# Block numbers of the expansion packed four to a word, one register load for 64 groups, column rows requested earlier

## The chip, the cores and the metric

The kernel runs on one core of one Trainium2 chip. The metric is the device time of one execution in microseconds (us); lower is better.

## What is computed

The reference is a three-layer graph network over N = 12,500 nodes with D = 128 features and E = 400,000 weighted edges.

```python
def _spmm(row, col, vals, x):
    msg = vals[:, None] * x[col]
    return jax.ops.segment_sum(msg, row, num_segments=N)

def _layer(x_prev, row, col, vals, W_a, b_a, W_b, b_b):
    h = _spmm(row, col, vals, x_prev)
    z = (h + x_prev) @ W_a.T + b_a + h * x_prev @ W_b.T + b_b
    return jnp.where(z >= 0, z, NEG_SLOPE * z)
x = emb[x_ids]
x1 = _layer(x, row, col, vals, W1_1, b1_1, W1_2, b1_2)
x2 = _layer(x1, row, col, vals, W2_1, b2_1, W2_2, b2_2)
x3 = _layer(x2, row, col, vals, W3_1, b3_1, W3_2, b3_2)
return jnp.concatenate((x, x1, x2, x3), axis=1)
```

## The kernel before

A preparation phase (the first third of the time) sorts the edges so that each layer can be computed with matmuls on blocks of 125 nodes, and writes small tables. Then a loop over the three layers (`with pe.Fori(0, LAYERS)`, line 956 on TensorE, and its like on the other engines) runs three stages after one another:

- **Expansion** (lines 960 to 973). The edges, ordered by the block of their source node, lie in 896 groups of 512 slots (GROUPS = 896, GE = 512). All edges of a group have their source in one block of 125 nodes. For a group TensorE makes the 512 messages as four tiles of 128 slots: each tile is a one-hot matrix of the column numbers (`col_hot`, the weights) times the block's features, which are split into three bf16 pieces (x_high, x_mid, x_low) summed in PSUM. So a group is 4 x 3 = 12 matmuls, each with its weight load. Which block a group uses is only known at run time. A loop body of AU = 16 groups (56 bodies a layer) begins with one instruction that loads 16 words from a table in SBUF (`group_at`, one word per group, already multiplied by D) into 16 registers of TensorE's sequencer (line 961), and each group's matmuls take their address from its register.
- Around it: SyncE loads the column numbers of 4 groups at a time (`load_cols`, line 636, one row of 4 KB, four rows in `col_src`), GpSimd spreads such a row to all partitions (line 556, into one of CR2 = 2 places in `col_row`), VectorE turns two groups at a time into one-hots (`make_hot`, line 1334, six groups ahead of use, a ring of OHR = 8 groups). PSUM has 8 banks, one group each. Of each pair of groups ScalarE multiplies the first by the edge values (line 745) and VectorE the second (line 1347) into a ring of MR = 8 message buffers, and SyncE stores each group, 128 x 512 fp32 = 256 KB, to memory (line 644).
- The order on SyncE's queue is written by hand in `store_messages`: before the stores of groups 0, 4, 8 and 12 of body i it waits for `col_spread[h]` (row h of body i has been spread, so its place in `col_src` is free) and loads row h of body i + 1.
- **Gather and sum** (lines 975 to 982): 592 tiles a layer; GpSimd gathers 128 rows of the stored messages by an indirect DMA (line 571), and TensorE sums them by rows with one-hot matmuls (line 980), a loop of 74 bodies of 8 tiles.
- **Dense** (lines 984 to 1018): the two weight matrices, the bias and the leaky step, written out for all 50 steps on TensorE without a loop, and the new features go to xb and to the output.

The tables are made once, in preparation: `start_groups` (line 1276) is written to memory as `group_offsets` by SyncE and read back as one row on partition 0 (lines 623 and 627).

Of the kernel before, what the change touches and what calls it, by code (L numbers as in the profile page):

```python
# [20 lines left out]
I32 = mybir.dt.int32  # L21
U8 = mybir.dt.uint8
ALU = mybir.AluOpType
# [3 lines left out]
P = 128  # L27
N = 12500
E = 400000
D = 128  # L30
LAYERS = 3
SLOPE = 0.2
DMA = 16
# [36 lines left out]
AU = 16  # L70
# [11 lines left out]
CR2 = 2  # L82
ABODIES = GROUPS // AU

CHB = 8
# [32 lines left out]
def graph_layers(nc, ids, row, col, vals, emb, weights, biases, out):  # L118
    ctx = ExitStack()
    with ctx:  # L120
# [6 lines left out]
        def dram(name, shape, dt=F32):  # L127
            return nc.dram_tensor(name, shape, dt, kind="Internal").ap()

        sorted_edges = [dram(f"sorted_edges{k}", [DUMPS[k] + SPARE, RUN * 2]) for k in range(2)]  # L130
        lane_places = dram("lane_places", [2, NBD, LT], BF16)
        group_offsets = dram("group_offsets", [P, GTW], I32)
        tile_rows = dram("tile_rows", [P, TBW], I32)
# [36 lines left out]
        iota_l = sb("iota_l", [P, TABW])  # L170
        start_groups = sb("start_groups", [P, GTW], I32)
        start_rows = sb("start_rows", [P, TBW], I32)
# [86 lines left out]
        base_of = work[:, TBL0 + TB:TBL0 + 2 * TB]  # L259
        group_at = wi[0:1, TBL0 + 2 * TB:TBL0 + 2 * TB + GROUPS]  # L260
        row_at = wi[0:1, TBL0 + 2 * TB + GROUPS:TBL0 + 3 * TB + GROUPS]
# [315 lines left out]
        def _(sp):  # L577
# [44 lines left out]
            sp.wait_ge(offsets_ready, 3)  # L622
            sp.dma_start(group_offsets, start_groups[:, :]).then_inc(offsets_stored, DMA)
            sp.dma_start(tile_rows, start_rows[:, :]).then_inc(offsets_stored, DMA)
            sp.dma_start(tile_base, start_base[:, :]).then_inc(offsets_stored, DMA)
            sp.wait_ge(offsets_stored, 3 * DMA)
            sp.dma_start(group_at, group_offsets.rearrange("p t -> (p t)")[0:GROUPS].rearrange("(a t) -> a t", a=1)).then_inc(offsets_in, DMA)
            sp.dma_start(row_at, tile_rows.rearrange("p t -> (p t)")[0:TB].rearrange("(a t) -> a t", a=1)).then_inc(offsets_in, DMA)
# [5 lines left out]
            with sp.Fori(0, LAYERS) as la:  # L634
                def load_cols(i, h):
                    sp.dma_start(col_src[h * 32:h * 32 + 1, :], cols_of[bass.ds(i * CB + h, 1), :]).then_inc(col_src_in[h], DMA)

                def store_messages(i, last):
                    for n in range(AU):
                        if n % BATCH == 0 and not last:  # L640
                            sp.wait_ge(col_spread[n // BATCH], la * ABODIES + i + 1)
                            load_cols(i + 1, n // BATCH)
                        sp.wait_ge(msg_ready[n % 2], la * (GROUPS // 2) + i * (AU // 2) + (ACREDIT + n // 2 + 1))
                        sp.dma_start(messages[bass.ds(i * (AU * P) + n * P, P), 0:CH * D], msg[:, n % MR, :]).then_inc(msg_stored[n % MR], DMA)  # L644

                for h in range(CB):
                    load_cols(0, h)
                with sp.Fori(0, ABODIES - 1) as i:
                    store_messages(i, False)
                store_messages(ABODIES - 1, True)  # L650
                with sp.Fori(0, DSTEPS // DU) as i:
                    for k in range(DU):
                        sp.wait_ge(xb_ready, la * DSTEPS + i * DU + (k + 2))
                        sp.dma_start(new_out[bass.ds(i * DU + k, 1), bass.ds(la + 1, 1), :, :, :].rearrange("a b r h d -> (a b r) h d"),
                                     xb[:, bass.ds(i * (2 * DU) + 2 * k, 2), :]).then_inc(x_stored, DMA)
# [138 lines left out]
        def _(pe):  # L794
# [161 lines left out]
            with pe.Fori(0, LAYERS) as la:  # L956
                pe.wait_ge(xb_ready, la * DSTEPS + 1)
                pe.wait_ge(pieces_ready, la * SPLITS + SPLITS)
                pe.sem_inc(pe_layers, 1)
                with pe.Fori(0, ABODIES) as i:  # L960
                    _, offs = nc.values_load_multi_w_load_instructions(
                        group_at[0:1, bass.ds(i * AU, AU)], engines=[mybir.EngineType.PE],
                        min_val=0, max_val=(NB - 1) * D, skip_runtime_bounds_check_because="the table holds offsets of blocks")
                    for n in range(AU):
                        if n % 2 == 0:
                            pe.wait_ge(col_hot_ready, la * (GROUPS // 2) + i * (AU // 2) + (n // 2 + 1))
                        pe.wait_ge(msg_ready[n % 2], la * (GROUPS // 2) + i * (AU // 2) + (n // 2 + 1))
                        for j in range(CH):
                            at = n % OHR * GE + j * P
                            for k, piece in enumerate((x_high, x_mid, x_low)):  # L970
                                last = t.matmul(ps[:, n % PR, j * D:(j + 1) * D], col_hot[:, at:at + P],  # L971
                                                piece[:, bass.ds(offs[n], D)], start=k == 0, stop=k == 2)
                        last.then_inc(expanded, 1)
# [47 lines left out]
        def _(dve):  # L1021
# [253 lines left out]
            blocks_of(iota_gt, GTW, ct[11][:, 0:NB], w[17][:, 0:GTW])  # L1275
            v.tensor_scalar(start_groups[:, :], w[17][:, 0:GTW], float(D), None, ALU.mult).then_inc(offsets_ready, 1)
            ask()
# [150 lines left out]
```

## Time and profile before

| | us |
|---|---|
| median of 3 runs | 8945.59 (8935.71 to 8948.48) |
| the profiled execution, its own time | 8948.78 |
| its span in the trace | 8947.1 |

```profile
PE 7924.2 (89%) x84296; PEld 7333.9 (82%) x84297; DVE 7107.3 (79%) x10046; ACT 4558.1 (51%) x14210; POOL 5595.2 (63%) x3638
PEclk8999995899996799999999999999999999999999
q8 instruction: 84, 1.38, 0.1%
PE 56%; DVE 5%; issue 3%; DMA 3%; ACT 1%; DVEq 1%; SPq 0%; POOL 0%; POOLq 0%; ACTq 0%
```

PE is TensorE's matmul side, PEld its weight loads, DVE VectorE, ACT ScalarE, POOL GpSimd. A q behind an engine's name is its sequencer or, for SP, its DMA queue. The first line gives busy time, share of the span and number of instructions; the second the granted clock of TensorE in 40 slices of the span, in tenths of full speed; the third the queue that carries instruction code (packets, MB, share of 16 engines); the last the shares of the chain that ended last. Register, branch and semaphore instructions are not counted as busy. A matmul's recorded end is modelled, so starts are the safer reading. In the rows of one line, a/b/c are the shortest, median and longest duration in ns, then the first and last start in us.

### The profile page before, as it was taken

The numbers are of one execution on the slowest core, as the hardware profiler recorded it, in microseconds if no ns is written. First come the engines' busy times: TensorE is split into PE (matmuls) and PEld (weight loads), VectorE is DVE, ScalarE is ACT, GpSimd is POOL, SyncE is SP. The second block draws the span as 40 slices with busy tenths as digits, with TensorE's granted clock in tenths as the row PEclk, the third lists the DMA queues.
The fourth block names the chain that finished last, engine by engine and source line by source line (L and its number), as shares of the span: only waits on it lengthen the run. The fifth ranks groups of instructions, "written<-read, shape, count | busy, mean of one in ns | idle before, by whom it ended". The sixth has DMA issues, their size and how long they took to land.

```text
span 8947.1 us, 257893 instructions
## 1 busy us (share of the span) xinstructions
PE 7924.2 (89%) x84296; PEld 7333.9 (82%) x84297; DVE 7107.3 (79%) x10046; ACT 4558.1 (51%) x14210; POOL 5595.2 (63%) x3638
## 2 busy tenths in 40 slices
PE   5999986799995688899999788899999788899999
PEld 4777775577773588799999788799999788899999
DVE  8999988799996877777777777777777777777777
ACT  0999990799993366611112566511112566511112
POOL 4788774588783233388886233488885333488884
PEclk8999995899996799999999999999999999999999
DMA  2111111211119988888886588888886688888885
GB/s 78 7 7 7 7 7 38 34 7 7 7 7 30 155 309 312 302 282 287 286 286 247 209 309 307 301 284 286 286 286 224 235 307 310 297 284 287 287 286 200
DMA packets 1005688, 1721.41 MB, mean 192 GB/s; under 512 B 378356, under 2 KB 429624, under 8 KB 1004920
## 3 DMA queue, kind: packets, MB, share of 16 engines
q0 software_dynamic: 378656, 958.17, 35.5%
q1 hardware_dynamic: 499680, 753.27, 23.7%
q10 hardware_dynamic: 127224, 8.24, 3.6%
q8 instruction: 84, 1.38, 0.1%
q14 instruction: 44, 0.36, 0.0%
HBM read 963.06 MB, written 756.12 MB: 192 GB/s over the span
## 4 chain that ended last, share of the span: by engine, by line
PE 56%; DVE 5%; issue 3%; DMA 3%; ACT 1%; DVEq 1%; SPq 0%; POOL 0%; POOLq 0%; ACTq 0%
PE ps L980 37%; PE ps L971 17%; DMA messages<-work 2%; DVE work L1334 2%; DVE hT L1297 1%; PE ps L1008 1%; PE ps L988 1%; PE ps L1009 1%; DVE work L1347 1%; ACT work L745 1%; SPq L644 0%; DVEq L1355 0%; PE ps L998 0%; DVE work L1321 0%; DVE hT L1359 0%
## 5 line engine op out<-in xcount | busy, mean ns | idle before, releaser
L980 PE MATMUL ps<-work 128*128 128x125 f32 x28416 | 3281.9, 278 | 45.8 <-DVE work L1363 45.5
L980 PEld LDWEIGHTS ps<-work 128*128 128x128 f32 x28416 | 3240.4, 192 | 87.2 <-DVE work L1363 46.9
L571 POOL DMA_INDIRECT work<-messages,work x1776 | 2708.8, 1525 | 615.9 <-issue 608.4
L971 PE MATMUL ps<-xb,work 125*128 x10752 | 1909.2, 222 | 450.8 <-DVE work L1334 426.3
L1363 DVE TENSOR_TENSOR work<-work,iota_p 128x1000 f32<-128x1000 f32 x1776 | 2120.0, 1194 | 0.4
L556 POOL PARTITION_BROADCAST work<-work x672 | 890.8, 1326 | 1854.9 <-DMA work<-slot_cols 903.6
L745 ACT ACTIVATE work<-ps,work 128x128 f32<-128x128 f32 x5376 | 1537.1, 369 | 960.4 <-PE ps L971 918.0
L971 PE MATMUL ps<-hT,work 125*128 x10752 | 1904.4, 221 | 0.0
L971 PE MATMUL ps<-work 125*128 x10752 | 1898.5, 220 | 0.0
L763 ACT ACTIVATE work<-work 128x8 f32<-128x8 f32 x1776 | 534.4, 301 | 2675.5 <-DMA work<-messages,work 2675.5
L870 PEld LDWEIGHTS ps<-hT 128*128 128x128 f32 x12768 | 1484.0, 196 | 297.1 <-ACT stage L668 227.3
L870 PE MATMUL ps<-hT 128*128 128x96 f32 x12768 | 1520.1, 280 | 186.6 <-ACT stage L668 186.3
L522 POOL DMA_INDIRECT sorted_edges<-stage,run_idx x798 | 1452.3, 1820 | 307.9 <-issue 237.5
L679 ACT ACTIVATE hT<-iota_p,place 128x128 f32<-128x128 f32 x5320 | 1580.2, 389 | 125.9 <-DVE place L1161 82.8
L971 PEld LDWEIGHTS ps<-xb,work 125*128 125x128 bf16 x10752 | 1047.0, 97 | 479.5 <-issue 479.5
L1347 DVE TENSOR_TENSOR work<-ps,work 128x512 f32<-128x512 f32 x1344 | 920.9, 685 | 636.0 <-PE ps L971 614.4
L1374 DVE TENSOR_TENSOR hT<-hT,ps 128x125 f32 x1776 | 505.8, 285 | 808.1 <-PE ps L980 808.1
L971 PEld LDWEIGHTS ps<-work 125*128 125x128 bf16 x10752 | 1046.6, 97 | 9.5
L971 PEld LDWEIGHTS ps<-hT,work 125*128 125x128 bf16 x10752 | 1052.4, 98 | 1.9
L1334 DVE TENSOR_SCALAR work<-work,iota_c 125x1024 bf16<-125x1024 bf16 x1344 | 885.8, 660 | 0.0
L1154 DVE TENSOR_REDUCE place<-ps 128x24 f32<-128x2400 f32 x266 | 706.5, 2656 | 110.1 <-ACT hT L682 96.6
L512 POOL TENSOR_TENSOR hT<-hT,work 128x672 f32<-128x672 f32 x266 | 363.2, 1366 | 428.6 <-DVE hT L1174 428.6
(212 smaller groups left out, 5680.8 us busy)
## 6 DMA issues: line engine op xcount, KB each, us to landing
messages<-work SPq DMA_DIRECT2D x2688, 256.0 KB, 3.2
work<-messages,work POOLq DMA_INDIRECT x1776, 5.9
out_x<-xb SPq DMA_DIRECT2D x150, 125.0 KB
sorted_edges<-stage,run_idx POOLq DMA_INDIRECT x798
work<-slot_cols SPq DMA_DIRECT2D x672, 4.0 KB
work<-lane_places SPq DMA_DIRECT2D x532, 5.2 KB, 2.1
out_x<-xb ACTq DMA_DIRECT2D x4, 1562.5 KB
sorted_edges<-hT SPq DMA_DIRECT2D x4, 908.0 KB
```

What stands on the lines that cost most here:

```text
L522: pool.indirect_dma_start(out=sorted_edges[p], out_offset=bass.IndirectOffsetOnAxis(ap=run_idx[:, q, k:k + 1], axis=0), in_=stage[:, q, k ...
L556: g.partition_broadcast(col_row[:, h % CR2, :], col_src[h * 32:h * 32 + 1, :], channels=P).then_inc(col_spread[h], 1)
L571: pool.indirect_dma_start(out=ck[:, n, :, :].rearrange("p h x -> p (h x)"), out_offset=None, in_=flat, in_offset=bass.IndirectOffsetOnAxis ...
L679: last = s.activation(to_part[q][:, k, :], iota_p[:, :], ACT.Abs, bias=place[:, q, 2, k:k + 1], scale=-1.0)
L745: last = s.activation(msg[:, n % MR, j * D:(j + 1) * D], ps[:, n % PR, j * D:(j + 1) * D], ACT.Copy, scale=val_now[:, n * CH + j:n * CH + ...
L870: last = t.matmul(ps[:, 6 + q, 0:2 * SLOTS], to_part[q][:, k, :], moved[q][:, k, :, :].rearrange("p f c -> p (f c)"), start=k == 0, stop=k ...
L971: last = t.matmul(ps[:, n % PR, j * D:(j + 1) * D], col_hot[:, at:at + P], piece[:, bass.ds(offs[n], D)], start=k == 0, stop=k == 2)
L980: last = t.matmul(part[n], ck[:, n, j // CH, j % CH * D:(j % CH + 1) * D], sel[:, n % SELB, j, :], start=j == 0, stop=j == CHB - 1)
L1154: v.tensor_reduce(at, ps[:, 0:BANKS, 0:BANKW].rearrange("p k (b l) -> p l k b", l=LANES), AX.XY, ALU.max).then_inc(rank_read, 1)
L1334: v.tensor_scalar(col_hot[:, n % OHR * GE:(n % OHR + 2) * GE], col_row[0:BLK, n // BATCH % CR2, n % BATCH * GE:(n % BATCH + 2) * GE], iota ...
L1347: v.tensor_tensor(msg[:, (n + 1) % MR, :].rearrange("p (j d) -> p j d", j=CH), ps[:, (n + 1) % PR, :].rearrange("p (j d) -> p j d", j=CH), ...
L1363: v.tensor_tensor(sel[:, n % SELB, :, :], row_rel[:, n, :][:, :, None].to_broadcast([P, CHB, BLK]), iota_p[:, 0:BLK][:, None, :].to_broadc ...
```

## The change

Four edits:

1. The table holds block numbers (0 to 99) as bytes, not offsets as 32-bit words: `start_groups` and its copy in memory become U8, VectorE copies in place of multiplying by D, and SyncE reads 896 bytes back in place of 3,584.
2. TensorE's loop body takes LB = 4 of the old bodies: 64 groups, written out, 14 times a layer. It loads 16 words for them, four block numbers in each.
3. Each group's offset is computed in registers, `((word >> 8k) & 255) * D`.
4. SyncE asks for a column row eight groups earlier than before: at groups 0 and 4 of body i rows 2 and 3 of body i + 1, at groups 8 and 12 rows 0 and 1 of body i + 2; rows 0 and 1 of body 1 are asked for ahead of the loop.

```diff
+LB = 4
-        group_offsets = dram("group_offsets", [P, GTW], I32)
+        group_blocks = dram("group_blocks", [P, GTW], U8)
-        start_groups = sb("start_groups", [P, GTW], I32)
+        start_groups = sb("start_groups", [P, GTW], U8)
-        group_at = wi[0:1, TBL0 + 2 * TB:TBL0 + 2 * TB + GROUPS]
+        group_at = wi[0:1, TBL0 + 2 * TB:TBL0 + 2 * TB + GROUPS // 4]
+        group_bytes = wu[0:1, 4 * (TBL0 + 2 * TB):4 * (TBL0 + 2 * TB) + GROUPS]
...
-                def store_messages(i, last):
+                def store_messages(i, left):
                     for n in range(AU):
-                        if n % BATCH == 0 and not last:
-                            sp.wait_ge(col_spread[n // BATCH], la * ABODIES + i + 1)
-                            load_cols(i + 1, n // BATCH)
+                        h = n // BATCH
+                        if n % BATCH == 0 and h < CR2 and left >= 1:
+                            sp.wait_ge(col_spread[CR2 + h], la * ABODIES + i + 1)
+                            load_cols(i + 1, CR2 + h)
+                        if n % BATCH == 0 and h >= CR2 and left >= 2:
+                            sp.wait_ge(col_spread[h - CR2], la * ABODIES + i + 2)
+                            load_cols(i + 2, h - CR2)
...
                 for h in range(CB):
                     load_cols(0, h)
-                with sp.Fori(0, ABODIES - 1) as i:
-                    store_messages(i, False)
-                store_messages(ABODIES - 1, True)
+                for h in range(CR2):
+                    sp.wait_ge(col_spread[h], la * ABODIES + 1)
+                    load_cols(1, h)
+                with sp.Fori(0, ABODIES - 2) as i:
+                    store_messages(i, 2)
+                store_messages(ABODIES - 2, 1)
+                store_messages(ABODIES - 1, 0)
...
-                with pe.Fori(0, ABODIES) as i:
-                    _, offs = nc.values_load_multi_w_load_instructions(
-                        group_at[0:1, bass.ds(i * AU, AU)], engines=[mybir.EngineType.PE],
...
-                    for n in range(AU):
+                with pe.Fori(0, ABODIES // LB) as i:
+                    _, four = nc.values_load_multi_w_load_instructions(
+                        group_at[0:1, bass.ds(i * (LB * AU // 4), LB * AU // 4)], engines=[mybir.EngineType.PE],
...
+                    for n in range(LB * AU):
+                        offset = ((four[n // 4] >> (n % 4 * 8)) & 255) * D
+                        offset.max_val = (NB - 1) * D
...
-                                                piece[:, bass.ds(offs[n], D)], start=k == 0, stop=k == 2)
+                                                piece[:, bass.ds(offset, D)], start=k == 0, stop=k == 2)
...
-            v.tensor_scalar(start_groups[:, :], w[17][:, 0:GTW], float(D), None, ALU.mult).then_inc(offsets_ready, 1)
+            v.tensor_copy(start_groups[:, :], w[17][:, 0:GTW]).then_inc(offsets_ready, 1)
```

## Rows read from the trace of the kernel before

**Rows 1.** Busy time by stage; then granted clock, DMA share, GB/s: expansion, then the rest.

```profile
3016.00:3782.00 766.00, 651.06 (x10752) 637.57 (x10752) 550.55 (x893) 526.49 (x1849) 290.20 (x222) 0.97 0.84 307
3782.00:5005.00 1223.00, 1170.93 (x9972) 1151.54 (x9972) 921.61 (x1350) 239.72 (x841) 908.42 (x595) 0.98 0.77 262
```

**Rows 2.** Groups by line, expansion of layer 1, 3030 to 3770 us (busy, mean ns, idle before).

```profile
L971 PE MATMUL ps<-xb,work 125*128 x3456 | 614.0, 223 | 112.0 <-DVE work L1334 102.1 <-issue 9.9
L1347 DVE TENSOR_TENSOR work<-ps,work 128x512 f32<-128x512 f32 x433 | 296.6, 685 | 204.3 <-PE ps L971 198.2
```

**Rows 3.** Timeline of TensorE at the end of one loop body.

```profile
3112.93 0.22 PE L971 MATMUL ps<-work 125*128 x1
3115.16 0.23 PE L971 MATMUL ps<-xb,work 125*128 x1 [2.01 <-DVE work L1334]
3115.33 0.22 PE L971 MATMUL ps<-hT,work 125*128 x1
3115.45 0.23 PE L971 MATMUL ps<-work 125*128 x1
```

**Rows 4.** Lines 961 and 960: all loads, one at a body's end, one after idle; the branches.

```profile
L961 PEldq TENSOR_LOAD <-work x168: 1103/2348/3118, 3014.3 to 7741.0; - x168
L961 PEldq TENSOR_LOAD <-work x1: 2243/2243/2243, 3112.5 to 3112.5; - x1
L961 PEldq TENSOR_LOAD <-work x1: 1103/1103/1103, 6990.6 to 6990.6; - x1
L960 PEldq COMPARE_BRANCH  x168: 76/213/227, 3028.8 to 7753.7; - x168
```

**Rows 5.** One line's instructions over 5003 to 5767.5 us, layer 2, line 971.

```profile
L971 PE MATMUL ps<-xb,work x3584: 219/219/314, 5005.5 to 5767.3; 125*128 x200
L971 PEldq FUSED_REGOPS  x1792: 51/53/60, 5005.4 to 5766.0; - x200
L971 PEldq ALU_OP  x896: 32/32/36, 5005.6 to 5765.9; - x180
```

**Rows 6.** The same line in the middle of one body, 3117.7 to 3125.9 us.

```profile
L971 PE MATMUL ps<-xb,work x49: 219/219/219, 3117.6 to 3125.8; 125*128 x49
```

**Rows 7.** One body at the lower clock and the next one, columns as in rows 1.

```profile
3100.50:3115.10 14.60, 12.61 (x192) 12.38 (x192) 9.46 (x16) 9.40 (x33) 5.28 (x4) 0.89 0.75 275
3115.10:3128.60 13.50, 11.30 (x192) 11.03 (x192) 10.17 (x16) 9.40 (x33) 5.20 (x4) 1.00 0.86 317
```

**Rows 8.** Line 956, the layer loop on TensorE: its branch back to the start, twice.

```profile
L956 PEldq COMPARE_BRANCH  x2: 3618/3729/3840, 4969.0 to 6955.2; - x2
```

**Rows 9.** The page's group of line 980, all three layers.

```profile
L980 PE MATMUL ps<-work 128*128 128x125 f32 x28416 | 3281.9, 278 | 45.8 <-DVE work L1363 45.5
```

**Rows 10.** DMA queues: 4969 to 4975 us, at the layer loop's branch (packets, MB, share).

```profile
q8 instruction: 2, 0.03, 2.1%
```

**Rows 11.** Line 967, a wait every two groups: right behind a load, and later.

```profile
L967 PEldq EVENT_SEMAPHORE  x2: 51/51/51, 3114.9 to 3116.0; - x2
L967 PEldq EVENT_SEMAPHORE  x5: 51/51/51, 3118.5 to 3124.0; - x5
```

**Rows 12.** Line 966 behind one load: the longest fused register instruction of a body.

```profile
L966 PEldq FUSED_REGOPS  x1: 108/108/108, 3114.8 to 3114.8; - x1
```

**Rows 13.** Waits of SyncE's queue, then of GpSimd, 3030 to 3770 us (us, times, longest).

```profile
SPq L644 <- ACT work L745: 84.7, 67, 2.5
SPq L644 <- DVE work L1347: 11.7, 30, 0.5
...
POOL work L556 <- DMA work<-slot_cols: 239.6, 130, 2.6
```

**Rows 14.** Single microseconds of one body, columns as in rows 1; line 644's landing times.

```profile
3119.00:3120.00 1.00, 1.00 (x21) 1.00 (x19) 0.72 (x3) 1.00 (x4) 0.32 (x1) 1.00 1.04 385
3131.00:3132.00 1.00, 1.00 (x21) 1.00 (x19) 0.88 (x3) 0.89 (x5) 0.00 (x0) 1.00 0.00 0
...
messages<-work SPq DMA_DIRECT2D x857, 256.0 KB, 3.3
```

More of the change, by code:

```diff
@@ L259, in graph_layers @@
         base_of = work[:, TBL0 + TB:TBL0 + 2 * TB]
-        group_at = wi[0:1, TBL0 + 2 * TB:TBL0 + 2 * TB + GROUPS]
+        group_at = wi[0:1, TBL0 + 2 * TB:TBL0 + 2 * TB + GROUPS // 4]
+        group_bytes = wu[0:1, 4 * (TBL0 + 2 * TB):4 * (TBL0 + 2 * TB) + GROUPS]
+        assert ABODIES % LB == 0 and NB <= 128
         row_at = wi[0:1, TBL0 + 2 * TB + GROUPS:TBL0 + 3 * TB + GROUPS]
@@ L622, in _ @@
             sp.wait_ge(offsets_ready, 3)
-            sp.dma_start(group_offsets, start_groups[:, :]).then_inc(offsets_stored, DMA)
+            sp.dma_start(group_blocks, start_groups[:, :]).then_inc(offsets_stored, DMA)
             sp.dma_start(tile_rows, start_rows[:, :]).then_inc(offsets_stored, DMA)
@@ L626, in _ @@
             sp.wait_ge(offsets_stored, 3 * DMA)
-            sp.dma_start(group_at, group_offsets.rearrange("p t -> (p t)")[0:GROUPS].rearrange("(a t) -> a t", a=1)).then_inc(offsets_in, DMA)
+            sp.dma_start(group_bytes, group_blocks.rearrange("p t -> (p t)")[0:GROUPS].rearrange("(a t) -> a t", a=1)).then_inc(offsets_in, DMA)
             sp.dma_start(row_at, tile_rows.rearrange("p t -> (p t)")[0:TB].rearrange("(a t) -> a t", a=1)).then_inc(offsets_in, DMA)
@@ L959, in _ @@
                 pe.sem_inc(pe_layers, 1)
-                with pe.Fori(0, ABODIES) as i:
-                    _, offs = nc.values_load_multi_w_load_instructions(
-                        group_at[0:1, bass.ds(i * AU, AU)], engines=[mybir.EngineType.PE],
-                        min_val=0, max_val=(NB - 1) * D, skip_runtime_bounds_check_because="the table holds offsets of blocks")
-                    for n in range(AU):
+                with pe.Fori(0, ABODIES // LB) as i:
+                    _, four = nc.values_load_multi_w_load_instructions(
+                        group_at[0:1, bass.ds(i * (LB * AU // 4), LB * AU // 4)], engines=[mybir.EngineType.PE],
+                        min_val=0, max_val=(NB - 1) * 0x01010101,
+                        skip_runtime_bounds_check_because="the table holds four numbers of blocks in each word")
+                    for n in range(LB * AU):
+                        offset = ((four[n // 4] >> (n % 4 * 8)) & 255) * D
+                        offset.max_val = (NB - 1) * D
                         if n % 2 == 0:
-                            pe.wait_ge(col_hot_ready, la * (GROUPS // 2) + i * (AU // 2) + (n // 2 + 1))
-                        pe.wait_ge(msg_ready[n % 2], la * (GROUPS // 2) + i * (AU // 2) + (n // 2 + 1))
+                            pe.wait_ge(col_hot_ready, la * (GROUPS // 2) + i * (LB * AU // 2) + (n // 2 + 1))
+                        pe.wait_ge(msg_ready[n % 2], la * (GROUPS // 2) + i * (LB * AU // 2) + (n // 2 + 1))
                         for j in range(CH):
```

## Prediction

> **What bounds the kernel now.** I read the busy time by stage first [rows 1]. A layer is an expansion of some 762 us and 1,220 us of gather, sum and dense. The change touches only the expansion and a small table in preparation, so the second stretch is out of the sum. In the expansion TensorE is busy 651 of 766 us, more than any other engine, and the DMA share is 0.84. Who waits for whom [rows 2]: TensorE is idle 112 of 740 us, VectorE 204 us and nearly all of it for TensorE. So TensorE leads. Its idle time is put down to VectorE's line 1334, but the timeline at the end of a body [rows 3] shows otherwise: the last matmul starts at 3112.93 and the next at 3115.16, and exactly there lies the register load, 2.24 us from 3112.5 [rows 4]. It starts 0.4 us ahead of the last matmul, since the sequencer is that far ahead, and the next body can't start without it. Loads that find TensorE idle take 1.10 us, those at a body's end 2.35 in the median, so over a microsecond of each waits for the matmuls in front to drain.
>
> In the middle of a body the matmuls run without a hole: 48 starts of one piece, so 144 matmuls, in 8.2 us [rows 6], 0.0569 us each. A layer's 10,752 take 612 us. The stage, 5005.5 to 5767.4 [rows 5], takes 762. The 150 us between are 55 body ends and the clock. One end costs 3115.16 - 3112.93 - 0.06 = 2.17, plus 0.19 for the first three matmuls, which start 0.12 to 0.17 apart; with the median load 0.1 longer than this one, 2.45. That makes 135. The other 15 us are clock: a body right behind an idle end with the granted clock at 0.89 took 14.6 us against 13.5 [rows 7]; in it matmuls run at the 1.2 GHz level for some 3 us. That is some 12 bodies a layer. 612 + 135 + 15 = 762: the sum closes with no wait inside a body.
>
> **The change part by part.**
>
> Loads: 14 in place of 56 a layer, so 13 ends between 64-group bodies in place of 55. At today's price the 42 removed ends are worth 42 x 2.45 = 103 us a layer.
>
> Branch: the loop body on TensorE grows fourfold, and this is the part that costs. Today it has 192 matmuls, 192 weight loads and 68 register instructions (48 on line 971 [rows 5], the rest waits, the load and the loop), 452. Four of them with one load and one loop are 4 x 448 + 4 = 1,796, before any unpacking. The branch back over 452 takes 0.21 us [rows 4]. The trace has one branch back over a span like the new one: the layer loop's, over 452 of expansion, the tile loop's 274 (28,416 / 222 bodies = 128 matmuls, as many loads, 18 others [rows 9]) and the dense stage, 9,972 - 9,472 = 500 matmuls, 500 loads [rows 1, 9] and some 150 waits: about 1,880. That branch took 3.62 and 3.84 us [rows 8], and beside it the instruction queue moved two packets of 16 KB [rows 10]. So TensorE's code isn't kept over such a distance; the start of the loop is fetched again. I take that for each new back-edge. It starts some 0.8 us ahead of the last matmul (load start 0.4, less branch and loop arithmetic), then comes the load, which now finds TensorE idle: 1.10 to 1.30. Last matmul to first of the next: -0.8 + 3.7 + 0.1 + 1.2 + 0.45 = 4.65, so 4.6 + 0.2 = 4.8 an end; the fetch now shares the DMA engines with a full stream of stores, which the layer's branch doesn't, for which I add 0.3 (0 to 1.4, a doubling of the fetch behind the overlap): 5.1. So 13 x 5.1 = 66 in place of 135: 69 us saved, not 103. Blocks met going forward are fetched ahead today without a hole in the dense stage, and cost nothing here.
>
> Here stands a rule of the Trainium skill, page Runtime: NRT & Kernel Launch, section Instruction fetch mechanics: TensorE's instruction memory holds 2,048 instructions, refilled in blocks of 256. By that size alone 1,796 could stay, and the sum would be the first rival's. The same section says that a taken branch whose target is outside of the current two pages must fetch it; by that the sum is mine. The branch of the layer loop [rows 8] bears out the second, over a span that would also fit the size.
>
> Unpacking: a shift and a mask more for each group, on the sequencer. Its slack: a wait that comes every two groups followed after 1.1 us when the queue was empty and every 1.37 us ((3124.0 - 3118.5) / 4) in steady state [rows 11]; so 0.14 us a group is free. A fused register instruction of 53 ns holds the present address [rows 5], the longest of the body takes 108 ns [rows 12]: if the two operations are fused into the first address, 0.02 to 0.055 us more, hidden, cost 0. If each of the three addresses repeats them fused, 3 x 0.055 = 0.165, 0.03 over the slack, 25 us a layer. I take 5, nearest to the first, since the rows show three instructions for three addresses, so shared work is shared today; 0 to 25 for the range.
>
> Clock: today some 12 of 55 ends are followed by a slow stretch of 1.1 to 1.3 us. The new ones are fewer but twice as long. From 4 (the same share of 13) to 13 x 1.3 = 17 or more; I take 16, as today.
>
> SyncE, stores and rings: SyncE waits only 85 + 12 us in 740 [rows 13], 13% of the time, and issues 857 stores in 730 us [rows 14]: 0.87 x 730 / 857 = 0.742 us of its own for a store, 665 us a layer, its stalls behind full DMA queues included. So it is no bound at 703 but would be the next one. DMA peaks at 385 GB/s [rows 14]: 235 MB a layer, 610 us. Inside 64 groups SyncE (0.742 or less) falls behind TensorE (0.683) by up to 3.5 us, landing takes 3.3 [rows 14], and 8 message buffers with 8 PSUM banks cover 10.9: I add 4 us a layer (0 to 13).
>
> Column rows earlier: nobody on the path waits for them. GpSimd waits 240 us for them [rows 13], yet TensorE has no wait inside a body. Worth 0, and 0 to cost: SyncE's new waits are for rows spread before it gets there, and the same number of loads. Behind them on its queue stand the stores; were a spread late, the 3.3 us of ring slack would cover it. The byte table: one copy for one multiply, a smaller read, 0, within 2 us either way.
>
> Sum, a layer: 612 + 66 + 16 + 5 + 4 = 703 against 762, 59 saved. Three layers: 177. 8948.8 - 177 = 8772 for an execution like the profiled one, which is 3 us above the median: 8769.
>
> **The rivals.**
>
> The code stays (chance 0.17). The back-edge costs today's price: 612 + 13 x 2.45 + 4 = 648, but then SyncE is late next at 0.742 a store with part of its stalls gone: 650 to 665. At 657, 105 a layer, 315 in all: 8631. For it: the new loop may be slightly shorter than the layer loop; against it: both branches of [rows 8].
>
> The sequencer becomes the bound, and the kernel slower (0.13). If shift, mask and multiply stay three instructions of their own at the pace of 1.1 us for some 9 register and wait instructions in two groups [rows 11], up to 0.12 each, a group takes 0.55 + 0.36 = 0.91, or 0.85 at 0.1 each: 762 for the matmuls, + 66 + 16 = 844, 82 more a layer: 9194. It decides from the point where a group takes 0.683 + 59 / 896 = 0.75, so from 0.20 us of added register work a group. For it: TensorE's sequencer is only 0.4 us ahead today. Against it: 0.14 free, and fused instructions exist.
>
> Fetch dearer or unpacking just over the slack (0.06): the ends at 6.5 to 8 with 25 to 30 for the unpacking, and the layer is back at 755 to 768: no change, 8940.
>
> That the change doesn't do what it says (the loads not fewer) has no opening in the diff.
>
> **How the numbers follow.** Forecast 0.64, at 8770: by its own ends (fetch +14, unpacking +20, rings +9, clock +10 a layer; below, the fetch -4, clock -12, the other two -9) 8700 to 8890. To hold 8 in 10 the range takes in most of the first rival: 8620 to 8890. Faster by over 0.2% (18 us, about what a measurement of this kernel can tell from no change): 0.64 + 0.17 and a little of the last, 0.82; same 0.05; slower 0.13.
>
> **What would show it.** Right: 42 loads on TensorE in all; branches of the expansion loop at 3.5 us or more in 39 of 42; many more instruction packets, some 8 for each back-edge, 300 and more; starts 0.057 apart in a body; hole of 4.5 to 5.5 at its end. Wrong: branches at 0.2 us; starts of a group's first matmuls more than 0.057 apart, which is the unpacking; waits on msg_stored by ScalarE or VectorE; SyncE never waiting.

## The result and the profile after

The changed kernel takes 8990.43 us in the median of five runs (8985.62 to 8993.09) against 8945.59 us: the ratio is 1.005, 95% interval 1.0036 to 1.0064. It is slower by 45 us, where 8769 was forecast.

The page of the changed kernel: engines, granted clock, and the queue of instruction code (packets, MB, share).

```profile
PE 8031.7 (89%) x84296; PEld 7389.7 (82%) x84297; DVE 7080.1 (79%) x10046; ACT 4539.3 (51%) x14210; POOL 5582.7 (62%) x3638
PEclk9999995899996799999999899999999899999999
q8 instruction: 453, 7.42, 0.4%
```

The matmuls are the same number, TensorE is 107 us longer busy with them, and the code queue moved 453 packets of 16 KB in place of 84. By stage (columns as in [rows 1]):

```profile
3012.00:3784.00 772.00, 682.82 (x10752) 651.34 (x10751) 544.09 (x891) 518.28 (x1839) 286.85 (x221) 0.94 0.84 305
3784.00:5011.50 1227.50, 1171.42 (x9972) 1152.41 (x9972) 923.08 (x1352) 242.25 (x850) 908.90 (x595) 0.98 0.78 262
```

The expansion went from 766 to 772 us and its granted clock from 0.97 to 0.94; the rest of the layer is within a few us. The lines that answer to [rows 4], branch and load of the expansion loop (shortest/median/longest, ns):

```profile
L971 PEldq COMPARE_BRANCH  x42: 76/4138/4400, 3060.2 to 7787.5; - x42
L972 PEldq TENSOR_LOAD <-work x42: 1117/1840/2444, 3010.0 to 7737.3; - x42
```

And to [rows 3]: the timeline of TensorE at one end between two bodies.

```profile
3115.58 0.22 PE L985 MATMUL ps<-work 125*128 x1
3121.94 0.29 PE L985 MATMUL ps<-xb,work 125*128 x1 [6.15 <-DVE work L1348]
3122.11 0.26 PE L985 MATMUL ps<-hT,work 125*128 x1
3122.22 0.29 PE L985 MATMUL ps<-work 125*128 x1
3122.30 0.31 PE L985 MATMUL ps<-xb,work 125*128 x1
```

The branch and then the load of the same end, the two lines from 3112 to 3123 us:

```profile
L971 PEldq COMPARE_BRANCH  x1: 4181/4181/4181, 3115.2 to 3115.2; - x1
```

```profile
L972 PEldq TENSOR_LOAD <-work x1: 1847/1847/1847, 3119.5 to 3119.5; - x1
```

To [rows 5], the register instructions of the matmuls' line in layer 2:

```profile
L985 PEldq ALU_OP  x2464: 36/36/41, 5012.0 to 5787.0; - x190
L985 PEldq FUSED_REGOPS  x1792: 51/58/69, 5012.1 to 5787.1; - x200
```

The branch runs from 3115.2 to 3119.4, the load from 3119.5 to 3121.4, the next matmul starts at 3121.94: 6.36 us from start to start where it was 2.23. Then the matmuls start 0.107 apart, the lower clock level. The unpacking is 2,464 register instructions on the line in place of 896, so 1.75 more for each group.

SyncE's waits for messages fell from 96 us to 31 (layer 1, 3020 to 3770 us), and ScalarE and VectorE now wait for stored messages (251 us together), which they did not before. SyncE's waits, then the two engines', then the stores' median landing on the page (us, times, longest; for the last the size and us):

```profile
SPq L651 <- ACT work L756: 22.1, 35, 1.6
SPq L651 <- DVE work L1361: 9.2, 18, 1.0
```

```profile
ACT work L756 <- DMA messages<-work: 138.3, 200, 2.3
DVE work L1361 <- DMA messages<-work: 112.9, 181, 2.0
```

```profile
messages<-work SPq DMA_DIRECT2D x2688, 256.0 KB, 4.0
```

**A balance of the stage.** From the starts of all 10,752 matmuls of a layer each kernel's stage can be split: the matmuls at 0.0569 us (611.7 us, the same for all); what the starts at the ends of bodies are further apart; the stretches at the lower clock (8 or more starts 0.08 to 0.2 apart in a row, single closer ones between them passed over); other single starts 0.08 to 0.2 apart, called short holes; starts 0.2 or more apart inside a body, called waits; and the widening of the normal spacing. Means of the three layers, us a layer:

| kernel | groups in a body | stage | ends | slow clock | short holes | waits | spacing |
|---|---|---|---|---|---|---|---|
| before | 16 | 763 | 124 | 19 | 7 | 0 | 2 |
| changed | 64 | 773 | 82 | 28 | 29 | 16 | 6 |
| long body alone | 64 | 802 | 89 | 32 | 5 | 63 | 2 |
| no unpacking | 64 | 708 | 25 | 10 | 20 | 38 | 4 |
| LB = 1 | 16 | 715 | 56 | 2 | 31 | 9 | 5 |
| LB = 2 | 32 | 716 | 40 | 2 | 36 | 20 | 6 |
| 56 groups | 56 | 744 | 75 | 27 | 16 | 10 | 4 |
| 56 groups, rows of 64 bytes | 56 | 717 | 41 | 20 | 25 | 16 | 4 |
| changed, old column order | 64 | 786 | 82 | 30 | 30 | 26 | 6 |
| LB = 1, old column order | 16 | 716 | 57 | 2 | 31 | 10 | 5 |
| changed, half stores | 64 | 757 | 74 | 32 | 25 | 8 | 6 |
| LB = 1, half stores | 16 | 682 | 44 | 2 | 19 | 0 | 5 |
| before, column order alone | 16 | 764 | 129 | 14 | 7 | 0 | 2 |
| before, unpacking alone | 16 | 843 | 151 | 60 | 16 | 0 | 4 |

In the row "no unpacking" four groups share a word (below); the rows with "half stores" are single runs. Before to changed: the ends give 41 us back, and clock (9), short holes (23), waits (16) and spacing (4) take 52. Ten us lost a layer, 30 in three; the profiled spans differ by 37.

### The profile page after: what moved, and what is told of

It reads as the page before. It is cut to its first block, busy times and chain, and to the rows that moved or that the text cites. A ratio compares the mean times of both kernels' runs of the same rounds, so it can differ in the third digit from the quotient of the medians.

```text
span 8983.8 us, 262132 instructions
## 1 busy us (share of the span) xinstructions
PE 8031.7 (89%) x84296; PEld 7389.7 (82%) x84297; DVE 7080.1 (79%) x10046; ACT 4539.3 (51%) x14210; POOL 5582.7 (62%) x3638
## 4 chain that ended last, share of the span: by engine, by line
PE 49%; ACT 18%; issue 11%; SPq 8%; DMA 7%; DVE 6%; ACTq 1%; POOL 1%; DVEq 0%; POOLq 0%
PE ps L994 36%; ACT hT L690 16%; PE ps L985 7%; SPq L651 6%; DMA messages<-work 6%; SPq L639 1%; PE ps L828 1%; DVE hT L1311 1%; DVE hT L1091 1%; DMA sorted_edges<-stage,run_idx 1%; PE ps L1022 1%; PE ps L1002 1%; PE ps L1023 1%; PE ps L855 1%; ACT work L756 1%
## 5 line engine op out<-in xcount | busy, mean ns | idle before, releaser
L985 PE MATMUL ps<-xb,work 125*128 x10752 | 1973.4, 224 | 375.1 <-DVE work L1348 245.5
L756 ACT ACTIVATE work<-ps,work 128x128 f32<-128x128 f32 x5376 | 1519.1, 370 | 1015.5 <-PE ps L985 565.7
L985 PE MATMUL ps<-hT,work 125*128 x10752 | 1974.0, 223 | 1.8
L985 PE MATMUL ps<-work 125*128 x10752 | 1961.1, 222 | 0.6
L1348 DVE TENSOR_SCALAR work<-work,iota_c 125x1024 bf16<-125x1024 bf16 x1344 | 840.0, 626 | 0.0
```

Source lines behind the costliest of these rows:

```text
L756: last = s.activation(msg[:, n % MR, j * D:(j + 1) * D], ps[:, n % PR, j * D:(j + 1) * D], ACT.Copy, scale=val_now[:, n * CH + j:n * CH + ...
L1348: v.tensor_scalar(col_hot[:, n % OHR * GE:(n % OHR + 2) * GE], col_row[0:BLK, n // BATCH % CR2, n % BATCH * GE:(n % BATCH + 2) * GE], iota ...
```

## The experiments

Each is compared with runs of the kernel before on the same chip (8948 to 8952 in the median). Two explanations run through the expectations. Theory A: the loss has three parts, the code fetched again at each branch back, the unpacking on TensorE's sequencer (27 us a layer of short holes and wider spacing), and waits of the rings. Rival B: the fetch is all of the loss and the unpacking costs nothing.

**Where the code is fetched again.** The kernel before with its body written out four times:

```diff
-                with pe.Fori(0, ABODIES) as i:
-                    _, offs = nc.values_load_multi_w_load_instructions(
-                        group_at[0:1, bass.ds(i * AU, AU)], engines=[mybir.EngineType.PE],
+                with pe.Fori(0, ABODIES // 4) as i4:
+                    for u in range(4):
+                        _, offs = nc.values_load_multi_w_load_instructions(
+                            group_at[0:1, bass.ds(i4 * (4 * AU) + u * AU, AU)], engines=[mybir.EngineType.PE],
```

> The kernel before with its expansion body written out four times (64 groups between branch and target), each part with its own load of 16 offsets, no bytes, no unpacking, the old order of the column rows. It measures the long body alone. Both theories: 13 branches a layer of 3.7 to 4.4 us in place of 0.2, the other 42 ends as before. Theory A: part of it overlaps the last matmuls, + 13 x 3.6 = 47, and some 8 of clock: 818 us a layer, 9110. If the new loss were not in the branch, this kernel would be at 8945 to 8960.

Measured 9076.84 us, ratio 1.0141 (1.0124 to 1.0158): 33 us under the 9110 expected, and far from the 8945 to 8960 of a loss that isn't in the branch. Branch and code queue of this kernel:

```profile
L960 PEldq COMPARE_BRANCH  x42: 76/4996/5809, 3061.8 to 7868.8; - x42
```

```profile
q8 instruction: 450, 7.37, 0.4%
```

Its body has 1,802 instructions, counted between two branches in the trace, and they are fetched again at every branch back. The stage is 39 us a layer longer, 127 us in all. That is a net price: the 13 ends with a fetch cost 89 us, where 13 ends of the kernel before cost 29, and the clock 13 more. But the other 42 loads now stand inside a body, without a branch. They are the 63 us of waits, 1.5 us each, where an end with its branch costs 2.25, so 32 us are given back.

The counterpart is the changed kernel without unpacking. Its table holds 32-bit offsets again, and four groups use one of them as it is, so most of its messages are made from another block's features:

```diff
-                        offset = ((four[n // 4] >> (n % 4 * 8)) & 255) * D
-                        offset.max_val = (NB - 1) * D
+                        offset = four[n // 4]
```

> The changed kernel without unpacking: four groups use one loaded 32-bit offset as it is, so most groups multiply with another block's features than the reference's; all instructions but the shifts, masks and multiplies stay, body of 64 groups, 16 words a load. Theory A: the short holes of 0.08 to 0.2 us between groups (some 270 a layer, 23 us) and the widened spacing (4 us) go, and the lead of the sequencer comes back at the 13 ends (0.4 us each): -30 a layer, 8900. Rival B (fetch alone): within 10 us of the changed kernel's 8990.

Measured 8789.33 us, ratio 0.9819 (0.9803 to 0.9835): 201 us under the changed kernel, where Theory A had 90 and Rival B under 10. Neither had this, in its branches and its code queue:

```profile
L971 PEldq COMPARE_BRANCH  x42: 76/208/226, 3058.6 to 7590.8; - x42
```

```profile
q8 instruction: 99, 1.62, 0.1%
```

The body is still 64 groups, yet its branches take 0.21 us. It is 1,536 matmuls and weight loads and 116 others, 1,652 against the changed kernel's 1,908, and that is short enough to be kept. Of the 256 instructions that are gone only 112 are the unpacking; the others formed an address for each group, and fewer do for four. Without those 112 alone the body would be 1,796 long, a length that no run has. So there is a length between 1,652 and 1,802 from which code is fetched again, and most of the 201 us is the code and not the time of the unpacking; how much, this run doesn't separate. A test of length alone, with all unpacking in place, is a body of 56 groups, some 1,670 instructions:

```diff
-LB = 4
+LG = 56
...
-                with pe.Fori(0, ABODIES // LB) as i:
+                with pe.Fori(0, GROUPS // LG) as i:
...
-                        group_at[0:1, bass.ds(i * (LB * AU // 4), LB * AU // 4)], engines=[mybir.EngineType.PE],
+                        group_at[0:1, bass.ds(i * (LG // 4), LG // 4)], engines=[mybir.EngineType.PE],
```

> The changed kernel with a body of 56 groups in place of 64 (16 bodies of 14 words, bytes and unpacking as they are): some 1,670 instructions from target to branch in place of 1,908. The runs so far have the code kept at some 1,650 and fetched again at 1,799. Theory A (length alone decides): branches of 0.21 us, 15 ends of 2.1 us after their start, 32 us a layer in place of 82, the slow clock behind them 5 in place of 28, the rest as in the run with 32 groups: 715 a layer, 8810 to 8825. Rival (the shared-word run kept its code for another reason, its missing unpacking or its few registers): branches over 3.5 us, 15 x 6.3, 9000 to 9020.

Measured 8906.28 us, ratio 0.9952 (0.9935 to 0.9969). The length theory is borne out, and the 8810 to 8825 expected of it is not: the code is kept, but the load of 14 words takes 4.5 us in the median. Branch, all loads, then the loads from 3050 to 3160 us and the single one at 3106.2:

```profile
L971 PEldq COMPARE_BRANCH  x48: 76/208/237, 3057.6 to 7706.3; - x48
L972 PEldq TENSOR_LOAD <-work x48: 1335/4460/6805, 3013.6 to 7657.7; - x48
L972 PEldq TENSOR_LOAD <-work x3: 2562/5717/6537, 3058.0 to 3151.2; - x3
L972 PEldq TENSOR_LOAD <-work x1: 2562/2562/2562, 3106.2 to 3106.2; - x1
```

Behind the first load of a layer long loads (5.7 to 6.8 us) and short ones (2.2 to 3.2) alternate through all three layers. A body's words begin 56 bytes after the last body's, so every second load begins 8 bytes off a multiple of 16, counted from the start of the table. The next run changes only where the words lie:

```diff
-        group_bytes = wu[0:1, 4 * (TBL0 + 2 * TB):4 * (TBL0 + 2 * TB) + GROUPS]
+        group_bytes = wu[0:1, 4 * (TBL0 + 2 * TB):4 * (TBL0 + 2 * TB) + GROUPS // LG * 64].rearrange("a (b t) -> a b t", t=64)[:, :, 0:LG]
...
-                        group_at[0:1, bass.ds(i * (LG // 4), LG // 4)], engines=[mybir.EngineType.PE],
+                        group_at[0:1, bass.ds(i * 16, LG // 4)], engines=[mybir.EngineType.PE],
```

> The body of 56 groups again, but each body's 14 words begin at a multiple of 64 bytes in the table (in the run before every second body's words began 56 bytes into a 64-byte stretch, and just those loads took 5.7 to 6.7 us, the others 2.2 to 2.8). Theory D (the load's address is the cause): all loads 1.3 to 2.6 us, 15 ends of 2.2 in place of 5.0, one in three with a slow stretch: 742 - 42 - 18 = 680 of its own, with the ring waits that then come 700 to 712 a layer, 8785 to 8815. Rival E (14 words are dear, or the code behind the load is late at the loop's start): loads stay at 6 us in every second body, 8906 as before.

Measured 8820.59 us, ratio 0.9854 (0.9838 to 0.987).

```profile
L972 PEldq TENSOR_LOAD <-work x48: 1343/2282/2954, 3017.6 to 7581.6; - x48
```

The address was the cause. The stage, 717 us, is a little over the 700 to 712 expected (and 8821 over 8785 to 8815), since slow stretches still follow most ends: 20 us, where one end in three, 5 to 8 us, was expected.

**The length of a load, without the long body.** One constant each:

```diff
-LB = 4
+LB = 1
```

> The changed kernel with LB = 1: bytes and unpacking stay, but the body is 16 groups again, with one load of 4 words in place of 16. Theory A (three costs: the fetched back-edge, the unpacking on the sequencer at some 27 us a layer in short holes, waits of the rings): no branch over 1 us here; if a load's time goes by its words (2.3 us for 16, so 0.6 to 1.2 for 4), the 55 ends save 45 to 60 us a layer, the unpacking takes 27, and the ring waits 10 at most: 8840 to 8900. Rival B (the fetch is all of the loss, unpacking free): the same saving without the 27: 8770 to 8815. If a load costs the same for 4 words as for 16, A says 9025 and B 8945.

> The changed kernel with LB = 2: 32 groups in a body, 28 bodies, 8 words a load, some 1,000 instructions between branch and target. Open is from which distance the code is fetched again. If it is kept: branches at 0.2 us, 27 ends of 2 us or less, 54 in place of 124 us a layer; Theory A then adds 27 for unpacking and 10 to 15 for ring waits: 725 to 735 us a layer, 8830 to 8860; Rival B without the unpacking 8760. If it is fetched: branches of 4 us, 27 x 6 = 160 us a layer of ends, 810 and more a layer, 9100 and more.

Measured 8811.13 us, ratio 0.9844 (0.9827 to 0.986), for LB = 1 and 8816.35, ratio 0.9851 (0.9834 to 0.9867), for LB = 2. Load and branch, LB = 1 and then LB = 2:

```profile
L972 PEldq TENSOR_LOAD <-work x168: 329/602/961, 3011.9 to 7601.2; - x168
L971 PEldq COMPARE_BRANCH  x168: 76/213/233, 3025.4 to 7613.2; - x168
```

```profile
L972 PEldq TENSOR_LOAD <-work x84: 588/1014/1360, 3010.8 to 7590.0; - x84
L971 PEldq COMPARE_BRANCH  x84: 76/213/237, 3036.5 to 7615.3; - x84
```

Both are under Theory A's ranges (8840 to 8900 and 8830 to 8860); LB = 1 is inside Rival B's. The balance still shows A's parts: against the kernel before LB = 1 saves 68 us a layer of ends and 17 of clock, more than A had, and loses 24 in short holes, 9 in waits and 3 in spacing. Packing with the old loop, unpacking included, beats both kernels. A load goes by its words: 4, 8 and 16 words take 0.60, 1.01 and 2.35 us beside the stores [rows 4] and 0.33, 0.59 and 1.10 where nothing is stored (the shortest, at a stage's start). And at ends of 1.1 us the clock stays up: one slow stretch a layer, at its start and behind no end (LB = 2 has none behind its 27 ends of 1.6 us either), against 10 to 12 of 55 ends of 2.3 us before.

**The unpacking by itself.** The kernel before, with the block's number times 256 in the table:

```diff
+                        offset = ((offs[n] >> 8) & 255) * D
+                        offset.max_val = (NB - 1) * D
...
-                                                piece[:, bass.ds(offs[n], D)], start=k == 0, stop=k == 2)
+                                                piece[:, bass.ds(offset, D)], start=k == 0, stop=k == 2)
...
-            v.tensor_scalar(start_groups[:, :], w[17][:, 0:GTW], float(D), None, ALU.mult).then_inc(offsets_ready, 1)
+            v.tensor_scalar(start_groups[:, :], w[17][:, 0:GTW], 256.0, None, ALU.mult).then_inc(offsets_ready, 1)
```

> The kernel before (16 groups, 16 words a load, old column order) with nothing but the unpacking added: the table holds the block's number times 256 and each group computes ((word >> 8) & 255) * D. Ring waits are absent here and the code is kept, so this is the unpacking alone. Theory A: the second and third matmul of every second group start 0.08 to 0.1 late (some 15 us a layer), the spacing widens (4), and the sequencer's lead at the 55 ends shrinks by 0.1 to 0.4 us each (5 to 20): 785 to 800 a layer, 9015 to 9060. Rival H (the unpacking is hidden and the short holes are echoes of ring waits): 8945 to 8965.

Measured 9187.14 us, ratio 1.0272 (1.0255 to 1.0289): 80 us a layer, twice of what the dearer theory had, 9015 to 9060. The short holes are small (10 us more than before, 2 more of spacing); what grew is the ends (124 to 151) and the slow clock (19 to 60). The expansion of layer 2 of this kernel, columns as in [rows 1]:

```profile
5065.00:5924.00 859.00, 708.82 (x10668) 692.04 (x10669) 543.77 (x892) 521.80 (x1831) 289.11 (x222) 0.89 0.74 271
```

The starts say how. Before, the load begins 0.45 us ahead of the last matmul of a body: the sequencer is that far ahead. With the unpacking it begins 0.07 ahead, and the first matmul follows 0.66 behind the load in place of 0.44. So an end is 0.5 us longer, 2.8 us in the mean, and 28, 47 and 32 of 55 of them in the three layers are followed by a slow stretch within 30 matmuls, in place of 12, 10 and 11.

**The message ring.** Half of each message stored, the rest of the program as it was; its totals can't be compared, as the other halves are written in preparation.

```diff
-                        sp.dma_start(messages[bass.ds(i * (AU * P) + n * P, P), 0:CH * D], msg[:, n % MR, :]).then_inc(msg_stored[n % MR], DMA)
+                        sp.dma_start(messages[bass.ds(i * (AU * P) + n * P, P), 0:CH * D // 2], msg[:, n % MR, 0:CH * D // 2]).then_inc(msg_stored[n % MR], DMA)
```

> The changed kernel (64 groups) storing only the first half of each message, 128 KB a group; the other halves are zeros written once in preparation, so its total isn't comparable, only the expansion stage (773 us). It takes the store queue away as a limit. Theory A: the waits of 0.2 us and more inside a body (16 us) go, the short holes between groups (29 us) are the unpacking and stay, the ends and the clock stay: 750 to 757. Rival C (the short holes are ring waits too): 725 to 732.

> The same halved stores with LB = 1; its stage was 715 us: 612 of matmuls, 56 of ends, 31 of short holes, 9 of longer waits, 5 of widened spacing. Theory A: 700 to 708 (only the longer waits go). Rival C (short holes are ring waits): 670 to 678.

The stages are 757 and 682 us. Landing of a store with LB = 1, all of it and then half of it (the second from 3300 to 3900 us):

```profile
messages<-work SPq DMA_DIRECT2D x2688, 256.0 KB, 4.9
```

```profile
messages<-work SPq DMA_DIRECT2D x790, 128.0 KB, 1.8
```

With LB = 4 the result is at the edge of Theory A's 750 to 757, and only half of its 16 us of waits are gone. With LB = 1 it is between the two theories: the 9 us of waits go, and 12 of the 31 us of short holes with them, and the ends fall by 12 because a load is faster beside lighter stores (0.33 us in place of 0.60). So of the short holes some 19 us stay without any wait, and 12 come with the ring waits. The balance bears this out from the other side: the kernel without unpacking has 20 us of short holes beside 38 of waits. SyncE issued as many stores as ever in these 682 us, so its issuing is not the limit that LB = 1 runs into; bytes and landing are.

**What the fetched code does to the stores.** In the changed kernel with half stores a store lands in 2.1 us and the DMA share is 0.48, and still ScalarE waits 91 us of 600 for stored messages; with LB = 1 and half stores it never does. SyncE's store issues of both from 3300 to 3900 us, LB = 4 and then LB = 1, and the code queue of the first in that window:

```profile
L654 SPq DMA_DIRECT2D messages<-work x705: 332/333/1727, 3299.3 to 3899.8; - x177
```

```profile
L654 SPq DMA_DIRECT2D messages<-work x790: 332/332/344, 3300.1 to 3899.7; - x198
```

```profile
q8 instruction: 99, 1.62, 1.4%
```

An issue takes SyncE 0.33 us, but some take over a microsecond. Counted over the three expansions of the run with LB = 4, 371 issues take more than 0.5 us, and 370 of them overlap one of the 372 packets of TensorE's code; with LB = 1 there are 6 such issues and 6 such packets. With full stores it is the same: in the changed kernel 366 of the 372 packets have an issue of more than 0.5 us beside them, and SyncE spends 472 us a layer on issuing, against 379 in the kernel before. The packets are spread over the whole body, one every 6 us in the mean. So a body that is fetched again pays for it in two places: TensorE at the branch, and SyncE by about a microsecond for each 16 KB all along, which delays the stores. Why an issue is held up, and how much of the changed kernel's 16 us of waits comes from this, no run separates.

Moving the even stores to ScalarE's queue was meant to ask the same in another way:

```diff
+                        if n % 2 == 0:
+                            continue
...
+                        act.wait_ge(msg_ready[0], la * (GROUPS // 2) + i * (AU // 2) + (ACREDIT + n // 2 + 1))
+                        act.dma_start(messages[bass.ds(i * (AU * P) + n * P, P), 0:CH * D], msg[:, n % MR, :]).then_inc(msg_stored[n % MR], DMA)
```

> LB = 1 with the stores of the even groups issued by ScalarE right behind its multiply, the odd ones by SyncE as before. It asks what the message ring waits for. Theory F (SyncE's issuing, 0.74 us a store, is the limit that LB = 1 runs into): ScalarE and VectorE wait less on stored messages, stage 715 falls toward the 682 of the halved stores: 685 to 695, 8720 to 8750. Theory G (the DMA engines' rate and landing time are, 329 GB/s at a share of 0.89): landing stays near 4.9 us, stage 705 to 720, 8780 to 8830.

Measured 9262.67 us, ratio 1.0349 (1.0332 to 1.0367), stage 867: outside of both theories. Landing fell to 2.6 us and the waits for stored messages went, but ScalarE, which now waits for its own multiply and issues the store before it goes on, became the slowest: its group of each pair takes 1.14 us of multiply and 0.67 of waiting and issuing, 1.81 together, and 448 pairs at that pace are 811 of the 867 us. SyncE's queue waits 404 us for VectorE's messages, which come in step with it. It says nothing on F against G.

**The column rows.** Edit 4 undone in the changed kernel and in LB = 1, and made alone in the kernel before (the diff of `store_messages`, backwards and forwards).

> The changed kernel with the old order of the column rows (edit 4 undone), 64 groups in a body. Theory A: edit 4 costs and gives nothing: within 10 us of the changed kernel's 8990. Rival: the 16 us a layer of waits inside the body come from SyncE standing in a wait for a spread row: then 8940 to 8955; or the rows come late without it: over 9010.

> LB = 1 with the old order of the column rows on SyncE (edit 4 undone). Theory A: edit 4 is worth nothing even with short ends: within 10 us of the 8811 of LB = 1. Rival: with less idle time at the ends the rows come late and VectorE waits for them: 8830 to 8900; or the earlier requests cost ring waits, then 8780 or less.

> The kernel before with edit 4 alone, the column rows asked for eight groups earlier. With LB = 4 the edit was worth 32 us, with LB = 1 8 us. Theory A: at today's ends of 2.3 us TensorE has no wait inside a body, so it is worth 0: 8940 to 8955. Rival: rows come late here too, unseen: 8925 or less.

Measured 9022.54 (ratio 1.0079, 1.0062 to 1.0096), 8818.77 (0.9855, 0.9838 to 0.9871) and 8948.72 (1.0001, 0.9992 to 1.0011). Alone the edit is worth nothing and with LB = 1 at most 8 us, both as Theory A had it. With the long body it is worth 27 to 32 us (by the ratios to the kernel before, and by the medians), where Theory A had none: the waits inside a body are 26 us a layer without it and 16 with it. GpSimd's waits for the rows in the changed kernel with the old order (layer 1, 3020 to 3760 us), where the kernel before has 240 us [rows 13]:

```profile
POOL work L559 <- DMA work<-slot_cols: 313.9, 158, 3.1
```

## Why the prediction was wrong

It had 703 us a layer and the stage takes 773. Of the 70 us between, the unpacking (5 forecast) and the end of a body are the larger part, then clock and rings. The closing balance of the kernel before held, and so did the mechanism on which the forecast turned: that a branch back over 64 groups fetches its code again. Step by step:

- **Loads and branches: right, with the branch mis-sized by little.** 42 loads; the branch 4.14 us where 3.7 plus 0.3 for the crowded DMA engines stood. The fetches, 453 - 84 = 369 more packets, are the "300 and more". But the forecast priced a fetch at the branch alone, and said that blocks met going forward cost nothing. On TensorE they cost nothing that the trace shows; SyncE's issues are held up beside them, which is in the rings' term.
- **The end of a body: mis-sized, 4.9 forecast without the start of the next body, 6.35 measured, 19 us a layer.** Two of its terms failed. The load was taken at 1.2 us, since loads of 2.35 were read as waiting for matmuls to drain. They don't: with TensorE long idle a load still takes 1.84, with half the stores 1.36 in the median, without any 1.10; and with LB = 1 and half stores a load that starts ahead of the last matmul takes the same 0.33 as at a stage's start. What stretches a load is the traffic of the stores. (The 0.5 us between 2.35 before and 1.84 here is not explained.) And the lead of the branch over the last matmul was taken at 0.8 us; with the unpacking it is 0.41, and 0.55 in place of 0.44 pass between load and first matmul.
- **Unpacking: the step that failed most.** It was priced by the sequencer's mean slack, 0.14 us a group, and put at 5 us (0 to 25). Mean slack was the wrong measure: mostly it is the second and third matmul of every second group, behind the wait for one-hots, that start late, and the lead over the last matmul is spent at each end, which is in the term above. Short holes and spacing grew by 27 us. That is the most that the unpacking can be charged with: where it was added alone, without ring waits, they grew by 12, and the rest comes with the waits. Against the kernel that has the long body without unpacking the short holes are 29 to 5. In the old loop the ends and the clock made it cost 80 us a layer.
- **Clock: 28 us where 16 stood.** The forecast said that longer ends might all be followed by a slow stretch, and took today's sum all the same. All 13 were, and the layer's start, for 2 us each.
- **Rings: 16 us where 4 stood (0 to 13).** SyncE and the landing fall behind in a body of 64 groups as said, but landing rose from 3.2 to 4.0 us (to 4.9 in the stages of 715 us), where the sum of ring and bank slack had 3.3, and SyncE's issuing rose by 93 us a layer beside the packets of code, which the sum didn't have. With half the bytes 8 of the 16 us are still there.
- **Column rows: 0 forecast, right for the kernel before and wrong for the changed one,** where the edit saves 27 to 32 us. A wait that isn't there in the kernel before was taken as absent in the changed one, whose bodies run 44 us without a pause and whose SyncE is held up by the fetches. Which of the two makes the rows late is not shown.
- **The rivals.** The first, that the code stays, had 8631; the runs in which it does stay (1,652 instructions, and 56 groups in rows of 64 bytes) are at 8789 and 8821. Its mechanism is real for bodies up to 1,670 instructions, 238 fewer than the changed kernel has. It promised too much: it took SyncE's 650 to 665 us as the next bound, and those two stages take 708 and 717, with 38 and 16 us of waits inside a body. The third, "fetch dearer or unpacking just over the slack, no change", given 0.06, is nearest to what happened, with its ends at 6.5. The slower rival had its point of decision at 0.20 us of added register work a group. The kernel is slower without reaching it: 1.75 register instructions of 36 ns are some 0.06 us. Ends, clock, unpacking and rings each came out above the forecast, and their sum did what the rival gave to one of them.

The prediction set a rule of the Trainium skill beside this (Runtime: NRT & Kernel Launch, Instruction fetch mechanics): TensorE's memory for 2,048 instructions, and a fetch for any branch whose target is outside of two pages of 256. The second part, which the prediction said the layer loop bears out, is not borne out: 1,652 and 1,670 instructions are more than six pages, and their branch takes 0.21 us. The first part fits if one page of the eight is being filled ahead: an estimate from that figure is 7 x 256 = 1,792, and it lies between 1,670, kept, and 1,802, fetched. No run here tried a length between those two, or moved the start of the loop within a page.

What is shown: a length between 1,670 and 1,802 instructions from which this loop's code is fetched again; the price of words, traffic and address of a load; the unpacking's effect on ends and, with them, on the clock; that SyncE's issues are long beside packets of code. What stays open: how the 27 us of holes and spacing and the 16 us of waits in the changed kernel divide between the unpacking, the held-up issues and the landing; and whether with LB = 1 the ring is bound by landing time or by the DMA engines' rate at 0.89 share, since more than 8 message buffers were not tried.

## What to carry to other kernels

Before a loop body is written out longer, count its instructions on that engine, registers and waits included, and leave room below the length from which a branch back fetches its code; here a body of 56 groups in place of 64, its words at good addresses, is worth 170 us. Where code is fetched again, look at the DMA issues of the other engines too. Of a removed pause ask what caught up in it: here an order of the column rows that cost nothing with 16 groups cost some 30 us with 64. And try the cheap half of a change alone: packing the words with the old loop gives 8811 us, 1.6% less than the kernel before, from three of the change's four edits.

## What the runs showed of the hardware

- A register load costs by the word, 0.07 to 0.08 us each in quiet (16 words in 1.10 us) and 0.13 to 0.15 beside full stores (16 in 2.35, 8 in 1.01), and 5.7 to 6.8 us for 14 words from an address 8 bytes off a multiple of 16, against 2.2 to 3.2 from a multiple.
- A branch back over 1,670 instructions takes TensorE 0.21 us, over 1,802 5.0 and over 1,908 4.1.
- Beside 366 of 372 packets of 16 KB of TensorE's code SyncE had a DMA issue of more than 0.5 us, where its median is 0.33: 93 us more of issuing a layer than in the kernel before. With half the stores it was 124 long issues a layer where code was fetched, and 2 where it was kept.
- TensorE fell to its lower clock level (starts 0.107 us apart) behind 0 of 55 idle ends of 1.1 us, 10 to 12 of 55 of 2.3 us, 28 to 47 of 55 of 2.8 us and all of 13 of 6.35 us, for 1.5 to 2 us of time each. Where the unpacking made the ends 27 us a layer longer, the clock took 41 us more.
